# Transformer layer on one core: order of the loads and of DVE's and ACT's work on the first eight token tiles

## The reference

```python
x = x + _layernorm(attn(_layernorm(x), q_w, k_w, v_w, o_w, q_b, k_b, v_b, o_b))
x = x + _layernorm(ffn(_layernorm(x), w_gate_up, w_down))
# attn: y = h @ w.T + b for q, k, v; scores = q k / sqrt(32), masked above the
#       diagonal; softmax; times v; @ o_w.T + o_b
# ffn:  gate, up = split(h @ w_gate_up.T); out = (silu(gate) * up) @ w_down.T
```

## Time and profile before

| | |
|---|---|
| median of 3 runs | 989.04 us (988.32 to 991.9) |
| the profiled execution | 990.02 us |
| its span in the profile | 988.2 us |
| busy share PE, DVE, POOL, ACT | 98%, 70%, 68%, 43% |
| share of the chain that ended last: PE, DVE, ACT, POOL, DMA | 85%, 8%, 2%, 2%, 1% |
| mean granted PE clock | 0.995 |

### The profile page before, as it was taken

How to read it: one execution, slowest core, us unless ns; L and a number is a source line. 1 busy time by engine, 2 the same in 40 slices (tenths; PEclk the granted TensorE clock), 3 DMA queues, 4 the chain that set the end, 5 groups by cost and what they waited for, 6 DMA issues and landing times.

```text
span 988.2 us, 15774 instructions
## 1 busy us (share of the span) xinstructions
PE 964.9 (98%) x5687; PEld 746.9 (76%) x5687; DVE 696.2 (70%) x1387; ACT 429.5 (43%) x761; POOL 668.2 (68%) x490
## 2 busy tenths in 40 slices
PE   7999999999999999999999999999999999999997
PEld 5766767777776677755878888888888888888885
DVE  7567788777796788776786777775827877777722
ACT  4566555555134555565344333322543433333242
POOL 5328888899328899962659766634886668666273
PEclk9999999999998999999999999999999999999999
DMA  7512233333413233231342211114332312211054
GB/s 244 161 49 77 77 80 83 87 95 88 128 62 77 76 82 87 66 93 37 137 139 77 94 65 64 64 43 150 87 116 97 107 64 86 86 65 65 24 158 138
DMA packets 49181, 90.69 MB, mean 92 GB/s; under 512 B 10448, under 2 KB 10960, under 8 KB 48848
## 3 DMA queue, kind: packets, MB, share of 16 engines
q1 hardware_dynamic: 48018, 88.66, 29.6%
q10 hardware_dynamic: 1086, 1.03, 0.4%
HBM read 55.84 MB, written 8.39 MB: 65 GB/s over the span
## 4 chain that ended last, share of the span: by engine, by line
PE 85%; DVE 8%; ACT 2%; issue 2%; POOL 2%; DMA 1%; SPq 0%; ACTq 0%; DVEq 0%; POOLq 0%
PE ps L1852 20%; PE ps L1853 20%; PE ps L1854 20%; PE ps L1951 8%; PE ps L1977 7%; PE ps L1924 6%; PE ps L2008 2%; PE ps L1959 1%; DVE stats L1642 1%; DMA x_in<-x 1%; DVE xt_lo L1462 1%; DVE stats L1647 1%; DVE ps L1485 1%; DVE p_sum L1440 1%; DVE firsts L1440 1%
## 5 line engine op out<-in xcount | busy, mean ns | idle before, releaser
L1485 DVE CUSTOM_DVE_ANT_0 ps<-ps,mask_q 128x384 f32<-128x384 f32 (+7 forms) x256 | 189.8, 780 | 55.9 <-PE ps L1924 53.5
L1951 PE MATMUL ps<-q_stack,k_stack 98*128 98x512 f32 (+3 forms) x384 | 114.0, 378 | 2.1 <-ACT x_in L1108 1.8
L1924 PE MATMUL ps<-k_stack,q_stack 96*128 96x512 f32 (+3 forms) x384 | 106.7, 360 | 1.6 <-DVE attn L1527 0.9
L848 POOL TENSOR_TENSOR dn_lo<-dn_raw,dn_hi 128x512 fp32r<-128x512 f32 x48 | 67.3, 1404 | 41.8 <-ACT dn_hi L1245 41.8
L1924 PEld LDWEIGHTS ps<-k_stack,q_stack 96*128 96x128 f32 x384 | 66.2, 191 | 26.9 <-DVE m_full L1485 10.9
L1951 PEld LDWEIGHTS ps<-q_stack,k_stack 98*128 98x128 f32 x384 | 62.3, 191 | 24.2 <-issue 6.2
L893 POOL TENSOR_TENSOR gu_lo<-s_raw,gu_hi 128x1024 fp32r<-128x1024 f32 x27 | 64.9, 2402 | 22.4 <-ACT gu_hi L1317 22.4
L1340 ACT ACTIVATE silu<-ps 128x512 f32<-128x512 f32 x27 | 16.2, 599 | 141.5 <-DVE ps L1743 141.5
L1108 ACT ACTIVATE p_own<-ps 128x512 f32<-128x512 f32 x112 | 61.0, 599 | 27.6 <-PE ps L1951 16.6
L1108 ACT ACTIVATE x_in<-ps 128x512 f32<-128x512 f32 x112 | 60.9, 598 | 27.8 <-PE ps L1951 15.4
L889 POOL TENSOR_TENSOR a_lo<-gu_raw,a_hi 128x512 fp32r<-128x512 f32 x27 | 35.9, 1331 | 52.0 <-ACT a_hi L1310 51.9
(11 more groups left out here) (241 smaller groups left out, 2750.3 us busy)
## 6 DMA issues: line engine op xcount, KB each, us to landing
gu_raw<-gu_w SPq DMA_DIRECT2D x37, 512.0 KB, 3.7
dn_raw<-dn_w SPq DMA_DIRECT2D x48, 256.0 KB, 2.6
k_stack<-st_hi SPq DMA_DIRECT2D x128, 64.0 KB, 2.0
q_stack<-st_hi SPq DMA_DIRECT2D x120, 64.0 KB, 2.0
x_in<-x SPq DMA_DIRECT2D x24, 256.0 KB, 4.8
qk_raw<-qk_w SPq DMA_DIRECT2D x16, 256.0 KB, 3.0
k_stack<-st_lo SPq DMA_DIRECT2D x64, 64.0 KB, 2.0
x_dram<-firsts SPq DMA_DIRECT2D x16, 256.0 KB, 2.0
```

Of the source, the lines that this page charges most:

```text
L848: nc.gpsimd.tensor_tensor(dn_lo[:, s], dn_raw[:, s], dn_hi[:, s].bitcast(F32), ALU.subtract).then_inc(dn_split, 1)
L1485: nc.vector.tensor_tensor_reduce(out=scores, in0=scores, in1=mask_q[:, SEQ - (t + 1) * P:], scale=1.0, scalar=MASKED, op0=ALU.add, op1=ALU ...
L1924: last = nc.tensor.matmul(bank[:, 0:width], q_stack[0:QK_ROWS, s, h, t * P:(t + 1) * P], k_stack[0:QK_ROWS, s, h, half * CH:half * CH + wi ...
L1951: last = nc.tensor.matmul(bank[:, at_col:at_col + n * P], k_stack[0:ROWS, s, h, kt * P:(kt + 1) * P], q_stack[0:ROWS, s, h, t * P:(t + n) ...
```

## The change

Four edits, all in the first stage:

- SP issues the load of tile 3 ahead of that of the value weights.
- `LAG_X` is 2 instead of 3: DVE does the low part of tile e - 2 in turn e.
- In START the first value product V 0 stands behind X 4 instead of ahead of it. Every user of the list follows.
- ACT makes the high parts of the value weights in turns 3 and 4 behind the tiles' high parts, instead of in turns 2 and 3 ahead of them.

```diff
-LAG_X = 3
-START = [("X", 0), ("X", 1), ("X", 2), ("X", 3), ("V", 0), ("X", 4), ("X", 5), ("P", (0, 0)), ("X", 6), ("X", 7), ("V", 1), ("P", (0, 1)),
+LAG_X = 2
+START = [("X", 0), ("X", 1), ("X", 2), ("X", 3), ("X", 4), ("V", 0), ("X", 5), ("P", (0, 0)), ("X", 6), ("X", 7), ("V", 1), ("P", (0, 1)),
...
                 load_x(n)
                 if n == 2:
                     load_qk(0)
+                elif n == 3:
                     sp.dma_start(vo_raw[:, 0], v_w).then_inc(vo_loaded[0], DMA)
                 elif n == 4:
                     sp.dma_start(v_bias[:, :], v_b.partition_broadcast(P)).then_inc(consts_loaded, DMA)
...
                 if e == 1:
                     hi_of_qk(0)
-                elif e in (2, 3):
-                    for k in range(KT // 2):
-                        hi_of_vo(0, vw_hi, (e - 2) * KT // 2 + k)
                 while e >= 2 and done < START.index(("M", 0)):
...
                     if START[done][0] == "X":
                         break
+                if e in (3, 4):
+                    for k in range(KT // 2):
+                        hi_of_vo(0, vw_hi, (e - 3) * KT // 2 + k)
```

## The result

Over 20 runs of each the changed kernel took 991.45 us in the median (990.31 to 994.22) and the kernel before 987.85 (986.69 to 991.9). The ratio is 1.0034, 95% interval [1.0028, 1.0040]: 3.4 us slower (2.8 to 4.0) by the ratio, 3.6 by the two medians. The forecast was 2.16 us slower and 991.2. The time is met to 0.3 us, but partly by luck: the median of 989.04 on which it stood came from three runs and lies 1.2 above that of the twenty, and the loss itself was put 1.2 too low. The profiled executions, 990.02 before and 990.49 after, are only 0.5 apart. That number alone would have shown almost no loss; why it is so small is the main thing to learn here.

The account below looks back on a forecast made before the run. PE's matmul queue was taken to bound the run, with DVE pacing its start. Delays of 0.4 (first value product's place) and 1.75 us (tile 7 behind the eviction) gave 989.04 + 2.16 = 991.2 us; range 988.0 to 994.4.

Parts of the forecast that it names:

- Part 1: SP's load queue: tile 3 lands at about 9.0 us, ahead of the value weights at 11.4.
- the yardstick: Start of the second value product on PE, 24.41 us in the profile before; its shift was taken as the change's price.
- Part 2: DVE's tile turns: tile 3's statistics at 10.63 instead of 11.43, turns 2.36 us instead of 2.04, tile 4's scaling delayed 0.36.
- The strict form of the rule: DVE and POOL exclude each other for whole instructions: tile 4's scaling would end at 17.50, the sum be 2.4 us.
- Part 3: PE's order: first value product at 17.69 behind 2.0 us idle, first projection at 20.94 instead of 20.52, 0.4 late.
- Part 4: DVE scales tile 7 behind the first projection's eviction: PE idle nearly 2 us, second value product at 26.57; 1.75 us lost.
- The sum: Second value product 2.16 us later, 0.4 from the first one's place and 1.75 from tile 7; 991.2 us forecast.
- Without waits: DVE's tile chain held up by nobody: second value product at 23.8, 0.6 us faster, 988.4; chance 0.10.
- Absorbed: PE's later waits for DVE, after 40 us, use up the delay: 989.0; chance 0.12.
- Clock, kind: The half-clock fall at 309.6 us does not come after the shift: 987.7; chance 0.08.
- Clock, adverse: New PE idle stretches of about 2 us bring a half-clock fall of seven us, costing 3.5: 994.7; chance 0.10.

Follow-up runs that it names:

- e3: Kernel before with only tile 3's load moved ahead and ACT's order changed (old lag, first value product ahead of tile 4); ratio 0.9987 to the kernel before.
- e10: Kernel before with only tile 3's load moved ahead of the value weights, ACT's order unchanged; ratio 1.0007 to the kernel before.
- e6: Changed kernel with tile 7 scaled ahead of the first projection's eviction and 16 unread matmuls ahead of tile 4's transposes; ratio 1.0012 to the kernel before.
- e1: Changed kernel with DVE scaling tile 7 ahead of the first projection's eviction; ratio 1.0023 to the kernel before.
- e5: Changed kernel with unread matmuls filling both new PE idle times, 16 ahead of tile 4's transposes and 14 ahead of tile 7's; ratio 1.0025 to the kernel before.
- e12: Changed kernel with LAG_X back at 3 and 16 unread matmuls ahead of tile 4's transposes; ratio 1.0000 to the kernel before.
- e8: Kernel before with 10 unread matmuls in round 1 of unit 8, where PE was not idle; ratio 1.0019 to the kernel before.
- e2: Kernel before with 15 unread matmuls ahead of the second value product, every order kept; ratio 1.0014 to the kernel before.
- e4: Changed kernel with LAG_X back at 3, first value product still behind tile 4; ratio 1.0001 to the kernel before.
- e11: Kernel before with tile 3's load and ACT's order changed, plus 10 unread matmuls in idle PE time before round 8 of unit 8; ratio 0.9985.
- e9: Kernel before, unchanged, profiled a second time; 986.29 us in one run.

## Why the prediction was right, and where it was off

**Part 1, the load.** Forecast landing at 9.0 with no wait for x_in behind it. In e3, where DVE comes earlier, the statistics begin at 9.43 without a wait, in e10 at 9.23. So it had landed by then; the 9.0 itself is in no row. The value weights, forecast for 11.4, came earlier: in e10 ACT waits for them until 10.00, and in the change (11.83) not at all. What the two transfers take was right, 10.00 - 6.91 = 3.09 us behind the projection weights against 0.65 + 2.4. The 8.35 on which they stood was that of a late execution, like the yardstick.

**Part 2, the turns.** Forecast 10.63 for tile 3's statistics and turns of 2.36; measured 10.22 and 2.35. The turn is right with its cause. The start is 0.41 early since tile 0's low part began at 9.61, not at 10.03: PE's transposes of tile 0 took 0.62 us here, where the row that I built on has 1.04, and ACT began the high part at 8.98. In e6, which has the change's order in this stretch, they took 1.06, and all came as forecast; its timeline of PE and, below it, that of DVE:

```profile
8.32 1.06 PE L1875 MATMUL ps<-ident,p_sum 128*128 128x128 f32 x4
```

```profile
10.04 0.69 DVE L1464 TENSOR_TENSOR xt_lo<-ps,xt_hi 128x512 fp32r<-128x512 f32 x1 [0.56 <-ACT xt_hi L1027]
```

Tile 3's statistics begin at 10.65 there and V0 at 17.66, against the 10.63 and 17.69 of the forecast. So these 0.4 us are a spread from execution to execution; why the four transposes take 0.6 or 1.04 to 1.06 us, at a granted clock of 1.00 both times, is not shown. The scaling of tile 4 was to be stretched by 0.36 under POOL's work and took 0.83 instead of 0.55, 0.28 more. The strict form of the rule that I had quoted from the Trainium skill (SBUF — State Buffer, "SBUF: two separate sides") would have DVE begin only when POOL's instruction ends. The timeline of POOL, after, has the two low parts whose second one runs beside that scaling:

```profile
13.76 2.70 POOL L900 TENSOR_TENSOR vw_lo<-attn,vw_hi 128x512 fp32r<-128x512 f32 x2
```

They end at 13.76 + 2.70 = 16.46, and the scaling ended 0.28 behind that, at 16.74, where a start at 16.46 and its own 0.55 would make 17.01. The measured row again decides against the strict form, as it did before with 0.29.

**Part 3, V0.** Forecast 17.69 with 2.0 of idle ahead, a wait of 0.6 at its eviction, P(0,0) at 20.94. Measured 17.27, 2.08, 0.66 and 20.46. The same 0.4 too late runs through; V0 then P(0,0) is 3.19 against 3.25.

**Part 4, the new wait.** Forecast eviction 24.71, scaling of tile 7 at 25.57, V1 at 26.57, PE idle for nearly 2 us. Measured 24.21, 25.07, 26.15 and 1.87. Right in each step, 0.4 to 0.5 early. In the profiles the term itself is met: P(0,0) to V1 is 5.69 us against 3.89 before, 1.80 more where I had 1.75. In time it is smaller, 1.1 us by e1 and 1.3 by e5 against e6, and so it is not the most of the loss, as the sum had it (1.75 of 2.16), but about half of what is left when the clock is filled away (2.5). The late turns of lag 2 cost about as much (e6 against e12, 1.2), which the early load did not make good.

**The sum: the step that was mis-sized.** "26.57 - 24.41 = 2.16": the first number was 0.4 too late and the second, as the mean of four landings has it, 0.7, and so the difference came out near the shift that was there. The term that was mis-sized is the yardstick: 24.41 is from an execution in which tile 3 landed late. With V1 at landing + 13.0 and the four landings read (10.07, 10.50, 10.96, 11.43, mean 10.74) it is 23.7. The change's V1 is 26.1 (26.15 and 25.99). That makes a shift of 2.4 (P(0,0), 0.06 earlier than in the first profile, is 0.6 later than with the mean landing, and the new wait adds the rest), and e5, the change without the falls at the start, pays 2.5 (1.6 to 3.5). The rest of the 3.4, about 1 us, is most likely the term that the sum put at nothing: half clock behind the new idle times. I had argued from 1.22 us of idle that "cost no clock"; e8, in the same order and with the same 1.22, has this in its view by stretch:

```profile
15.00:18.00 3.00, 2.72 (x9) 2.34 (x10) 2.93 (x8) 0.78 (x2) 1.35 (x1) 0.50 1.00 300
```

Three us at half clock. One row at full clock did not prove that the idle time is free. How the loss parts between shift and clock is not settled more closely than this: e5's interval holds 2.2 as well as 3.4, and e12 found nothing to win.

**The rivals.** "Without waits" is out: tile 7's transposes began at 25.77, not before 24.0. "Absorbed" is out: 1.77 at the first scores, 1.68 at 310 us, and e2 pays 1.4 for a shift of 1.55. "Clock, kind" happened in the profiled execution (3.4 instead of seven us at half clock) but not in the median; the kernel before has executions with and without the fall. "Clock, adverse" was right in its place (e1) and too dear in its price for unit 8: I had 3.5 us for seven us at half clock, by halving the speed, and they cost 2.3. What a fall costs depends on its place. At 310 us, from the scores to the mark, 3.4 us at half clock cost 0.8 to 1.2 (122.3 to 122.7 us in seven profiles, 121.5 to 121.6 in the six without a fall). Over V0 in e1 3.4 us cost 1.58. At 440 to 450 us, in e4, e10 and e11, they cost 1.6: from the mark to the end of the span it is 556.3 us, against 554.6 to 554.7 in nine of the other profiles (in e5 and e12 it is 0.8 longer with no fall in view, for a reason that is not shown). So it is a quarter to a third of the length at 310 and near a half elsewhere; why is not shown.

**Why the best version isn't better still.** From tile 3's statistics to V1 it is 13.2 us in e3 and 22.93 - 9.23 = 13.7 in e11, against 13.0 before: part of the earlier load is lost again. The timeline of PE, e3, has the next bound:

```profile
13.75 0.47 PE L1853 MATMUL ps<-vw_hi,xt_hi 128*128 128x512 f32 x1
...
15.73 0.50 PE L1853 MATMUL ps<-vw_hi,xt_hi 128*128 128x512 f32 x1 [0.28 <-POOL vw_lo L900]
...
17.15 0.50 PE L1853 MATMUL ps<-vw_hi,xt_hi 128*128 128x512 f32 x1 [0.46 <-POOL vw_lo L900]
...
17.96 1.03 PE L1874 MATMUL ps<-ident,p_sum 128*128 128x128 f32 x8
```

V0 begins at 13.75 and takes until 17.96, 4.21 us instead of 2.84, since it now waits for POOL's low parts of the value weights. V0's start, 2.40 us earlier than in the first profile, covers that; it is what is late next.

## What to carry to other kernels

A load that PE's chain waits for may be brought forward, but the engine that answers it in program order decides what that is worth: move the load together with the order of the engines behind it (e3), not alone (e10), and look which eviction a shorter lag puts ahead of the last tile's work (e1). A yardstick from one profile can be off by the spread of a DMA's landing; before a forecast of 2 us is built on it, ask which wait in that profile ends with a transfer and what the yardstick would be if it landed earlier. Where PE's new idle time is filled, put the fillers exactly where the trace shows PE idle: ten matmuls in the wrong round, with the wait for their bank, cost 1.9 us.

## What the runs showed of the hardware that was not expected

The same load behind the same queue landed between 10.07 and 11.43 us in four executions of one order, always 3.06 to 3.12 us behind an earlier load of the same queue. The granted clock was at half (1.2 GHz) behind idle times of 1.22 (e8), 1.29 (before), 2.08 (e1) and 2.54 us (e10), and stayed at 2.4 GHz behind 1.22 (before), 1.27 (e9), 2.08 (the change) and 2.07 (e4): the length of the idle time alone did not tell which. At 310 us the stretch at half clock was seven us in one execution and 3.4 in another. The same 3.4 us cost 0.8 to 1.2 us at 310 us, 1.58 over V0 (e1) and 1.6 at 440 to 450 us (e4, e10, e11).
